# Down projection of five of eight token blocks in seven products per pair of row tiles, with GpSimd making the operand sums

## The reference

```python
scale = cond @ norm_w.T + 1.0
h = x * (scale[:, None, :] * rsqrt(mean(x * x) + EPS))
val, gate = split(h @ up_w.T, 2)                 # 4096 x 2048 each
h = val * gelu(gate)
hq = act_quant(h)       # per token: round(h * 127 / max|h|) / scale
wq = weight_quant(down_w)                        # -1, 0 or 1, times one mean
return hq @ wq.T + x                             # 4096 x 512, float32
```

## Time and profile before

| | us |
|---|---|
| median of 3 runs | 743.75 (743.3 to 743.89) |
| profiled execution, its own time | 744.86 |
| its span in the profile | 743.0 |
| TensorE matmul busy | 733.5 (99%) |
| VectorE busy | 521.8 (70%) |
| ScalarE busy | 337.3 (45%) |
| GpSimd busy | 104.8 (14%) |

### The profile page before, as it was taken

The page is one execution under the profiler, slowest core; times in us unless marked ns, Lnnn a source line. Parts: engine busy times, 40 slices in busy tenths (PEclk is TensorE's granted clock), DMA queues, the critical chain, the costliest instruction groups (busy, mean ns, idle before and its releaser), DMA issues.

```text
span 743.0 us, 14261 instructions
## 1 busy us (share of the span) xinstructions
PE 733.5 (99%) x5506; PEld 539.1 (73%) x5506; DVE 521.8 (70%) x1006; ACT 337.3 (45%) x662; POOL 104.8 (14%) x153
## 2 busy tenths in 40 slices
PE   6999999999999999999999999999999999999998
PEld 6544444444688887888778886788878887788864
DVE  5567777875889666876578855787568855577556
ACT  4788856442355533364234542355324443244410
POOL 1211477787330000000000000000000000000000
PEclk9999999999999999999999999999999999999999
DMA  8887574757545453343634344343543334353202
GB/s 313 289 279 230 187 271 147 260 169 257 207 146 160 143 194 123 118 151 102 198 99 154 117 141 156 113 157 101 162 143 104 101 100 134 115 181 108 90 29 86
DMA packets 44564, 117.60 MB, mean 158 GB/s; under 512 B 5584, under 2 KB 5840, under 8 KB 43344
## 3 DMA queue, kind: packets, MB, share of 16 engines
q1 hardware_dynamic: 44496, 116.68, 47.8%
HBM read 99.88 MB, written 16.79 MB: 157 GB/s over the span
## 4 chain that ended last, share of the span: by engine, by line
PE 97%; DMA 1%; DVE 0%; issue 0%; POOL 0%; SPq 0%; ACT 0%; DVEq 0%; POOLq 0%
PE ps_v L589 14%; PE ps_v L588 14%; PE ps_v L590 14%; PE ps_y L716 13%; PE ps_g L589 6%; PE ps_g L588 6%; PE ps_g L590 6%; PE ps_v L606 4%; PE ps_g L607 4%; PE ps_g L606 4%; PE ps_v L607 4%; PE ps_v L608 4%; PE ps_g L608 4%; PE ps_v L795 1%; DMA q<-in_up_t_dram 1%; PE ps_v L682 1%
## 5 line engine op out<-in xcount | busy, mean ns | idle before, releaser
L588 PE MATMUL ps_v<-x_hi,w_hi 128*128 128x256 f16 x968 | 263.9, 273 | 0.0
L589 PE MATMUL ps_v<-x_lo,w_hi 128*128 128x256 f16 x968 | 263.9, 273 | 0.0
L590 PE MATMUL ps_v<-x_hi,w_lo 128*128 128x256 f16 x968 | 263.9, 273 | 0.0
L814 ACT COPY ps_g<-ps_v 128x256 f32<-128x256 f32 x96 | 34.3, 357 | 208.2 <-PE ps_v L590 208.2
L825 ACT ACTIVATE g<-ps_g,w_unscale 128x512 f32<-128x512 f32 x128 | 87.3, 682 | 77.6 <-PE ps_g L590 73.5
L1146 DVE TENSOR_TENSOR ps_v<-ps_v,p 128x256 f32<-128x256 f32 x96 | 41.5, 432 | 113.2 <-PE ps_v L590 113.0
L588 PE MATMUL ps_g<-x_hi,w_hi 128*128 128x256 f16 x392 | 106.9, 273 | 0.2 <-DVE x_lo L1136 0.2
L589 PE MATMUL ps_g<-x_lo,w_hi 128*128 128x256 f16 x392 | 106.9, 273 | 0.0
L590 PE MATMUL ps_g<-x_hi,w_lo 128*128 128x256 f16 x392 | 106.9, 273 | 0.0
L589 PEld LDWEIGHTS ps_v<-x_lo,w_hi 128*128 128x128 f16 x968 | 94.7, 98 | 13.5
L588 PEld LDWEIGHTS ps_v<-x_hi,w_hi 128*128 128x128 f16 x968 | 94.7, 98 | 13.5
(11 more groups left out here) (137 smaller groups left out, 889.6 us busy)
## 6 DMA issues: line engine op xcount, KB each, us to landing
w_lo<-w_lo_dram SPq DMA_DIRECT2D x96, 448.0 KB, 3.3
q<-in_up_t_dram SPq DMA_DIRECT2D x16, 512.0 KB, 4.4
xt<-in_x_cols_dram SPq DMA_DIRECT2D x8, 1024.0 KB, 4.9
res<-in_x_rows_dram SPq DMA_DIRECT2D x26, 256.0 KB, 3.4
out_dram<-res SPq DMA_DIRECT2D x26, 256.0 KB, 2.7
xs<-in_x_rows_dram SPq DMA_DIRECT2D x22, 256.0 KB, 3.6
w_lo_dram<-w_lo SPq DMA_DIRECT2D x16, 256.0 KB, 4.3
dw<-in_down_t_dram SPq DMA_DIRECT2D x8, 512.0 KB, 6.5
```

What stands on the lines that cost most here:

```text
L588: pe.matmul(to, w_hi[:, wh:wh + P], hi, start=start and kt == 0, stop=False, skip_group_check=True)
L589: pe.matmul(to, w_hi[:, wh:wh + P], lo, start=False, stop=False, skip_group_check=True)
L590: last = pe.matmul(to, w_lo[:, wl:wl + P], hi, start=False, stop=(kt == 1), skip_group_check=True)
```

## The change

The quantized activations q and the ternary weights dw are small integers, so sums and differences of them are exact. For blocks 2 to 5, and for one pair of block 6, two row tiles at a time (a pair: tiles 0 and 2, then 1 and 3) take seven block products of 8 matmuls with 256 columns, in place of 32 matmuls with 512.

- GpSimd makes four differences of dw once (`down_terms`, 2048 elements per partition each), three sums per pair of q tiles (`sum_tokens`, eight times a block, 256 elements each) and one more sum per pair (`sum_last`, 1024 elements).
- A pair is spread over four chunks: `d_pair` (16 matmuls) at the end of chunk j = 11 or 15, `d_second` (8) in the next, `d_third` (8) and `d_gates` (16) in the one after, `d_fourth` (8) in the fourth. Between them ScalarE makes two copies (`d_copies`) and VectorE two additions (`d_seed`, `d_second_low`) of 256 columns.
- The residuals come two at a time, in passes j = 14 and j = 2; the loads and stores of x rows and out rows move with them on SyncE's queue.
- Behind the loop only two row tiles of block 6 remain, and `spread_scale` of the last block stands in the middle of the second.

```diff
+    D_SEVEN = range(2, NB - 1)
+    D_START = 11
+    HD = D // 2
+    NK = J // 2
+    K_ORDER = [*range(1, NK), 0]
+    PAIR = ((0, 2), (1, 3))
+    def d_pairs(b):
+        return 2 if b < NB - 2 else 1
+    def d_chunk(n, since):
+        b, j = divmod(n - since, J)
+        b -= 1
+        return [(c, p) for c, p, at in ((b, 0, D_START), (b, 1, D_START + 4))
+                if c in D_SEVEN and p < d_pairs(c) and j == at]
...
+                if b - 1 in D_SEVEN and j == 15:
+                    store_y(b - 1, 0)
+                    store_y(b - 1, 1)
+                if b - 2 in D_SEVEN and j == 0:
+                    load_res(b - 2, 2)
+                    load_res(b - 2, 3)
...
+            def d_pair(b, p):
+                pe.wait_ge(ds_step, 3 * NK * (x + 1))
+                pe.wait_ge(y_done, b * TT + 2 * p)
+                d_product(d_low(0), q_parts[:, :, 0, 0, p, :], d_b[:, :, 0, 0, :], start=True)
+                d_product(d_low(1), d_s1[:, p], d_t[:, 0]).then_inc(dp_ready, 1)
+            def d_second(b, p):
+                pe.wait_ge(dp_copied, 2 * (2 * d_index(b) + p + 1))
+                d_product(d_low(0), d_s2[:, p], d_t[:, 1]).then_inc(du2_ready, 1)
...
+            def d_gates(b, p):
+                d_product(d_high(0), q_parts[:, :, 1, 0, p, :], d_b[:, :, 1, 0, :])
+                pe.wait_ge(ds4_ready, 2 * d_index(b) + p + 1)
+                d_product(d_high(1), q_parts[:, :, 0, 0, p, :], d_b[:, :, 1, 1, :]).then_inc(y_ready, 1)
...
-                if b >= 2 and j < 3:
+                for c, p in d_chunk(n, 0):
+                    d_pair(c, p)
+                for c, p in d_chunk(n, 2):
+                    d_gates(c, p)
+                if b >= 2 and b - 2 not in D_SEVEN and j < 3:
                     down(b - 2, j + 1)
...
-            down(NB - 2, 1)
+            down(NB - 2, 2)
             turn_max(NB - 1)
-            down(NB - 2, 2)
+            down(NB - 2, 3, range(NK))
             spread_scale(NB - 1)
-            down(NB - 2, 3)
+            down(NB - 2, 3, range(NK, J))
...
+            def sum_tokens(b, k):
+                pool.wait_ge(q_ready, b * J + Q_AT[2 * k + 1] + 1)
+                pool.tensor_tensor(d_s1[:, 0:r, k, :], a21, a22, ALU.add).then_inc(ds_step, 1)
+                pool.wait_ge(ds_step, base + 1)
+                pool.tensor_tensor(a21, a11, a21, ALU.subtract).then_inc(ds_step, 1)
+                pool.tensor_tensor(d_s2[:, 0:r, k, :], d_s1[:, 0:r, k, :], a11, ALU.subtract).then_inc(ds_step, 1)
```

More of the change, by code:

```diff
@@ L196, in bass_cond_norm_geglu_bitlinear @@
         scale_all = tb[:, 1, TB // Q:2 * (TB // Q)]
+        d_t = dw_room[:, J * D // 2:].bitcast(FP8).rearrange("p (t k n) -> p t k n", t=4, k=NK)
+        d_b = dw.rearrange("p (k o h n) -> p k o h n", k=NK, o=2, h=2)
+        d_s1 = sums[:, 0:WS].bitcast(FP16).rearrange("p (r k n) -> p r k n", r=2, k=NK)
+        d_s2 = sums[:, WS:2 * WS].bitcast(FP16).rearrange("p (r k n) -> p r k n", r=2, k=NK)
+        q_parts = q[:].rearrange("p (k o h r n) -> p k o h r n", k=NK, o=2, h=2, r=2)
+        d_copy = [sums[:, p * WS // 2:p * WS // 2 + HD] for p in range(2)]
         cond_sb = p5[:, 0, 0:B]
@@ L308, in bass_cond_norm_geglu_bitlinear @@
         y_ready = sem("y_ready")
+        dt_step = sem("dt_step")
+        ds_step = sem("ds_step")
+        ds4_ready = sem("ds4_ready")
+        dp_ready = sem("dp_ready")
+        dp_copied = sem("dp_copied")
+        du2_ready = sem("du2_ready")
+        dg_seeded = sem("dg_seeded")
+        du3_ready = sem("du3_ready")
+        dv2_ready = sem("dv2_ready")
         y_done = sem("y_done")
@@ L706, in spread_scale, with down @@
                 last.then_inc(scale_rows, 1)
-            def down(b, i):
+            def down(b, i, part=range(J)):
+                r = y_row(b, i)
                 if i == 0:
@@ L757, in _ @@
                     down(b - 2, 0)
+                for c, p in d_chunk(n, 1):
+                    d_second(c, p)
+                for c, p in d_chunk(n, 2):
+                    d_third(c, p)
+                for c, p in d_chunk(n, 3):
+                    d_fourth(c, p)
                 if seven:
@@ L777, in _ @@
                     spread_scale(b - 1)
-                if b >= 1 and j == J - 1 and n + 1 != 2 * J:
+                if b >= 1 and b - 1 not in D_SEVEN and j == J - 1 and n + 1 != 2 * J:
                     down(b - 1, 0)
@@ L817, in copies, with d_copies @@
                 act.copy(p5[:, sevens(n) % 2, :], ps_v[:, n % NV, HB:TB]).then_inc(pair_copied, 1)
+            def d_copies(b, p):
+                act.wait_ge(dp_ready, 2 * d_index(b) + p + 1)
+                act.copy(ps_y[:, 1, 0:HD], ps_y[:, 0, 0:HD]).then_inc(dp_copied, 1)
+                act.copy(d_copy[p], ps_y[:, 0, HD:D]).then_inc(dp_copied, 1)
             def gelu(n):
@@ L912, in _ @@
                 b, j = divmod(n, J)
+                for c, p in d_chunk(n, 1):
+                    d_copies(c, p)
                 if n < NJ and in_seven(n):
@@ L1029, in _, with down_terms, sum_last @@
                 sum_weights(k)
+            def down_terms():
+                b11, b12, b21, b22 = [d_b[:, :, i // 2, i % 2, :] for i in range(4)]
+                pool.wait_ge(ws_ready, J)
+                pool.tensor_tensor(d_t[:, 0], b12, b11, ALU.subtract, saturate=False).then_inc(dt_step, 1)
+                pool.wait_ge(dt_step, 1)
+                pool.tensor_tensor(d_t[:, 1], b22, d_t[:, 0], ALU.subtract, saturate=False).then_inc(dt_step, 1)
+                pool.tensor_tensor(d_t[:, 2], b22, b12, ALU.subtract, saturate=False).then_inc(dt_step, 1)
+                pool.wait_ge(dt_step, 2)
+                pool.tensor_tensor(d_t[:, 3], b21, d_t[:, 1], ALU.subtract, saturate=False).then_inc(dt_step, 1)
+            def sum_tokens(b, k):
+                x = d_index(b)
+                base = 3 * (NK * x + K_ORDER.index(k))
+                r = d_pairs(b)
+                a11, a21, a22 = [q_parts[:, k, o, half, 0:r] for o, half in ((0, 0), (0, 1), (1, 1))]
+                pool.wait_ge(q_ready, b * J + Q_AT[2 * k + 1] + 1)
+                if x >= 1:
+                    pool.wait_ge(dv2_ready, 2 * x)
+                pool.tensor_tensor(d_s1[:, 0:r, k, :], a21, a22, ALU.add).then_inc(ds_step, 1)
+                pool.wait_ge(ds_step, base + 1)
+                pool.tensor_tensor(a21, a11, a21, ALU.subtract).then_inc(ds_step, 1)
+                pool.tensor_tensor(d_s2[:, 0:r, k, :], d_s1[:, 0:r, k, :], a11, ALU.subtract).then_inc(ds_step, 1)
+            def sum_last(b, p):
+                x = d_index(b)
+                pool.wait_ge(dp_ready, 2 * x + p + 1)
+                pool.wait_ge(ds_step, 3 * NK * (x + 1))
+                pool.tensor_tensor(q_parts[:, :, 0, 0, p, :], q_parts[:, :, 1, 0, p, :], d_s2[:, p],
+                                   ALU.subtract).then_inc(ds4_ready, 1)
+            down_terms()
+            for b in D_SEVEN:
+                for k in K_ORDER:
+                    sum_tokens(b, k)
+                for p in range(d_pairs(b)):
+                    sum_last(b, p)
         @block.vector
@@ L1321, in _ @@
                     peak_of(n - 2)
-                if b >= 2 and j < 4 and n < NJ:
+                if b >= 2 and b - 2 not in D_SEVEN and j < 4 and n < NJ:
                     residual(b - 2, j, ps_y[:, j % 2, :])
+                for c, p in d_chunk(n, 3):
+                    residual(c, 2 * p, ps_y[:, 1, :])
                 if n < NJ and in_seven(n):
                     seed_gate(n)
+                for c, p in d_chunk(n, 1):
+                    d_seed(c, p)
+                for c, p in d_chunk(n, 2):
+                    d_second_low(c, p)
+                for c, p in d_chunk(n, 3):
+                    residual(c, 2 * p + 1, ps_y[:, 0, :])
                 if 1 <= b < NB and j == 2 and by_vector(b - 1):
```

60 lines of the change are left out of this document (48 added, 12 removed).

## The result

| | before | changed |
|---|---|---|
| median | 743.57 us, 8 runs (743.3 to 743.89) | 748.36 us, 8 runs (745.14 to 748.73) |
| ratio | | 1.0052, 95% interval 1.004 to 1.0065: slower by some 0.5% |
| profiled execution, span | 744.86, 743.0 | 745.14, 743.3 |

The ratio is an estimate from the single times; the quotient of the two medians is 1.0064. The forecast was 745.3, in a range of 741 to 750. The measured median lies in that range, but 3.1 us above the forecast, and outside the 743 to 747 of the likeliest case alone. The eight times of the changed kernel fall in three groups: one of 745.1, two of 746.6, five of 748.3 to 748.7 us. Their mean granted TensorE clocks are 1.0, 0.998 and 0.995. The profile is of the one at 1.0, so it shows what the waits do, and not what the clock does.

The account below looks back on a forecast made before the run. TensorE, busy for 99% of the span, was taken to bound the kernel. Savings of 7.1 us against waits of 6.5, 0.8, 0.8, 0.4 and 0.1 gave +1.5 us: 743.75 to 745.3 us, range 741 to 750.

Parts of the forecast that it names:

- the likeliest case: TensorE waits for ScalarE's late copies in chunk j = 3, blocks 4 to 6; 743 to 747 us, chance 0.50.
- The products: Down projection: seven products of 8 half-width matmuls save TensorE 0.79 us for each of 9 pairs, 7.1 us.
- The hand-offs of the pairs: Copies and additions between a pair's chunks cost nothing, being covered by 3.3 us and more of matmuls.
- The cover: Chunk j = 3: shorter cover makes TensorE wait 2.2 us in blocks 4 to 6, 6.5 in all; block 7 0.8.
- GpSimd's long differences: `down_terms`, from 232.9 us on: a VectorE maximum waits behind the first instruction, delaying a seed; 0.8 us.
- GpSimd's sums: Sums meeting VectorE instructions in passes j = 4, 5, 7 and 10 just fit the slack; 0.4 us in all.
- The two meetings of pass 4: Pass j = 4, blocks 3 to 6: XT2 and a `low` each meet GpSimd, 1.1 us longer together, just fitting.
- Late sums: Rival: GpSimd's sums at 1.59 us each fall behind and TensorE waits five times; 758 us, chance 0.10 for above 754.
- The end: Last seed in chunk 127 costs 0.03 us; `spread_scale` after `turn_max` fits by 0.4 us, so nothing.
- The sum at full clock: All terms for the whole kernel added: -7.1 + 6.5 + 0.8 + 0.8 + 0.4 + 0.1 = +1.5 us.
- other rivals: Enough cover, 737 to 742 us, 0.20; GpSimd holding VectorE beyond its slack, 747 to 754, 0.20; sums too late, above 754, 0.10.

Follow-up runs that it names:

- cast_later: Changed kernel with only ScalarE's cast of XT1 moved from pass j = 2 to j = 4 (blocks 3 to 6): 743.23 us, ratio 0.9996.
- res_later: Changed kernel with only the residual of a block's last row tile moved from VectorE's pass j = 2 to j = 3: 742.72 us, ratio 0.9989.
- xt1_later: Changed kernel with difference XT1 and its cast moved from pass j = 2 to j = 3 (blocks 3 to 6): 741.74 us, ratio 0.9974.
- all_later: Changed kernel with XT1 and last residual in pass 3, XT1's cast in pass 4, `down_terms` in 32 pieces: 740.63 us, ratio 0.9959.
- before_waits: Kernel before the change, with XT1's cast made seven times in blocks 4 to 6 so TensorE stands still: 749.99 us, ratio 1.0086.

## Why the prediction was right, and where it was not

- **The products.** 0.79 us a pair, 7.1 us in all, was right: the medians lie 0.0 to 0.6 us above the sum in every row of the table.
- **The hand-offs of the pairs cost nothing.** Right: no wait for them in any profile.
- **The cover.** The likeliest case was the right mechanism at the right place and of the right size: 2.25 us against 2.18, three times; cast_later showed that it was ScalarE's order, res_later that the second residual was 0.65 of it, xt1_later that without both XT1 and its cast block 7's size (0.65, measured 0.77) is left. `second_val` behind it, 1.25 worked out in the expectation of cast_later, was 1.38. These three stands came out 0.07 to 0.13 us longer than worked out.
- **GpSimd's long differences.** 0.8 us, measured 0.89, by the mechanism named. The Trainium skill's rule ("SBUF — State Buffer", "Who interferes with whom"), that the second to come waits until the other is done, agrees with the trace: the maximum took 1.67 us more beside one instruction and ended 0.55 us behind it. The Trainium skill's "GPSIMD Engine Reference", section 3.1, has 4497 ns for 2048 fp32 elements; here 2048 fp8 elements took 3.83 to 4.28 us, and no run has the fp32 instruction.
- **GpSimd's sums.** 0.4 us was put for them; they cost nothing in the changed kernel. The two meetings of pass 4 were put at 1.1 us; they were 0.6 (XT2 0.82 us and not 1.2, `low` 1.15). The four `dequant` instructions of pass 5, 0.96 us longer beside GpSimd, were not in the prediction at all. Nothing came of either in the changed kernel, where VectorE had 0.99 us to spare ahead of pass 4. all_later, with XT1 and the residual in pass 3, had none and paid 0.8 us a block, taken back by moving one `low`.
- **Late sums.** Not seen: the sums of 256 elements took 0.67 to 1.12 us, and TensorE waited for none.
- **The end.** 0.04 us at the last seed, against 0.03 worked out, and no wait behind `turn_max`.
- **The sum at full clock.** The stands add to 8.6 us and the terms to 8.6 too, but in part by luck: 6.75 against 6.5, 0.89 against 0.8 and 0.92 against 0.8 were too small by 0.5 us together, and GpSimd's 0.4 was nothing.
- **What failed: the sum itself, which had no term for the clock.** It stopped at "+1.5 us" and took TensorE's wait of 2.2 us to cost 2.2 us. It cost 1.7 us more in most executions, once or twice in each. That is why the median is 3.1 us above the forecast while the profile is as forecast, and why a change put on the border between no difference and slower came out slower, clear of the noise. The median still lies in 741 to 750 only because that range was widened for other rivals: it is outside the 743 to 747 given for the forecast's own mechanism, and 747 to 754 had been put down to GpSimd, which had no part in it. That the range holds is luck. With waits shorter by 0.2 us, as in before_waits, the clock might have stayed, and the forecast's 745 would have been near the median.

What stays open: why one stand of 2.25 us is followed by half clock and the next, of the same length to 0.01 us, is not; and why behind three stands of 2.7 us it was two times and not three. I did not try lengths between 2.04 and 2.25, nor the same length of stand in both kernels.

## What to carry to other kernels

Where work of TensorE is cut, look at what it had been hiding: here two engines' passes were fitted under row tiles of 3.45 us, and a good change came out slower until four instructions were moved by one or two passes and four long ones were split. Work out the path between two hand-offs from both sides, engine by engine, with the instruction that merely stands in front in a queue counted in full. A still stand of TensorE in the midst of full load has two prices, its length, and a stretch at half clock once it gets long (here 1.7 us more behind some of those of 2.25 us, and none up to 2.04). Short ones cost their length alone.

## What the runs showed of the hardware that was not expected

- TensorE, busy without a break before, stood still for 1.6 us (res_later, clock 0.999 or more in eleven runs) and for 2.04 us without losing its clock; after 2.25 us it was granted half in 12 of 13 executions of the changed kernel, one or two times in each by their times and clocks (18 falls for 39 stands), and after 2.7 us in all four, by the clock of 0.995 two times for three stands in each. In the three falls that were profiled, the clock fell 0.6, 0.6 and 1.2 us after the matmuls had begun again, and stayed at half for 3.4 us, which costs 1.7 us. The profile of a single execution, at clock 1.0, showed none of it: only the list of runs did.
- Four small VectorE instructions (32 x 4 elements, with one scalar per partition in place of a second tensor) took 1.92 us while GpSimd was making sums, and 0.96 us in the kernel before, where GpSimd was idle.
- GpSimd's `tensor_tensor` of 256 fp16 elements took 0.67 us at the least and up to 1.12, of 1024 elements 2.12 to 2.37 us.
